# Patch tokens made for all images at the front, and a new order in the attention bodies

## What is computed

```
x = patches(img)                          # 32 x 36 rows of 768
x = layernorm(x) * ln1_g + ln1_b
x = x @ W_lin + b_lin                     # 768 -> 192
x = layernorm(x) * ln2_g + ln2_b
h = concat(cls, x) + pos                  # 37 image tokens an image
h = concat(h, txt)                        # 165 tokens an image
h = h + linear_attention(layernorm(h))    # scores without softmax
h = h + block(layernorm(h))               # 12 heads with softmax, MLP, mixture of 4 experts (top 2)
```

## Time and profile before

| what | value |
|---|---|
| runs, median | 1278.51 us (1276.96 to 1279.22) |
| profiled execution: span | 1279.6 us |
| TensorE (PE) busy | 1201.2 us, 94% |
| VectorE (DVE) busy | 939.3 us, 73% |
| ScalarE (ACT) busy | 730.0 us, 57% |
| GpSimd (POOL) busy | 412.7 us, 32% |

### The profile page before, as it was taken

One profiled execution on the slowest core, in us unless ns is written; L12 is line 12 of the kernel. 1 busy time (PEld: TensorE's weight loads), 2 busy tenths in 40 slices (PEclk: granted clock), 3 DMA queues, 4 the chain that ended last, 5 costly groups with the idle time before them and its releaser, 6 DMA issues.

```text
span 1279.6 us, 28412 instructions
## 1 busy us (share of the span) xinstructions
PE 1201.2 (94%) x9894; PEld 1025.9 (80%) x9894; DVE 939.3 (73%) x2602; ACT 730.0 (57%) x1705; POOL 412.7 (32%) x397
## 2 busy tenths in 40 slices
PE   7899999999999999999998899999999999999994
PEld 6777777777777777777776799998888899899993
DVE  4677787777777787778767678777778877776773
ACT  1256555555566545655557655554656666667661
POOL 2101110111111110111010027877568644455444
PEclk8899999999999999999999999999999999999997
DMA  3481122202120122112400524346477677667652
GB/s 106 122 214 37 38 64 56 64 16 57 56 64 21 51 64 57 39 34 64 96 18 9 206 47 81 79 90 159 118 190 196 169 179 183 164 159 171 183 143 30
DMA packets 95387, 124.51 MB, mean 97 GB/s; under 512 B 9382, under 2 KB 87591, under 8 KB 91343
## 3 DMA queue, kind: packets, MB, share of 16 engines
q1 hardware_dynamic: 71743, 102.48, 26.7%
q0 software_dynamic: 23568, 21.06, 10.9%
HBM read 70.68 MB, written 52.83 MB: 97 GB/s over the span
## 4 chain that ended last, share of the span: by engine, by line
PE 61%; DVE 13%; issue 10%; POOL 5%; DMA 5%; ACT 5%; DVEq 0%; POOLq 0%; SPq 0%; ACTq 0%
PE PS L1634 49%; PE PS L1637 12%; DMA out<-YO,ids 4%; POOL out L769 2%; DVE K L1182 2%; POOL expert_rows L732 1%; DVE st L1094 1%; DVE rec L1204 1%; ACT PT L787 1%; DMA consts<-in_attn_const 1%; ACT XAT L787 1%; ACT GF L980 1%; DVE CN L1205 1%; ACT PX L812 1%; DVE ZS L1152 1%
## 5 line engine op out<-in xcount | busy, mean ns | idle before, releaser
L1634 PE MATMUL PS<-w2r,GH 128*120 (+1 forms) x828 | 247.6, 362 | 2.4 <-DVE GL L1359 1.2
L659 POOL TENSOR_TENSOR rs<-ve,minus_half 128x3 f32<-128x3 f32 (+1 forms) x80 | 58.8, 736 | 558.6 <-DVE ve L1099 558.6
L769 POOL DMA_INDIRECT out<-YO,ids x94 | 160.9, 1712 | 147.0 <-DVE flag L1575 64.0
L1634 PE MATMUL PS<-w2r,GL 128*120 (+1 forms) x828 | 208.0, 251 | 0.0
L812 ACT ACTIVATE PX<-PS,nb 128x165 f32<-128x165 f32 x576 | 177.1, 417 | 47.6 <-DVE nb L1170 45.9
L980 ACT ACTIVATE GF<-PS,b1c 128x480 f32<-128x480 f32 (+1 forms) x216 | 137.8, 638 | 81.9 <-PE PS L1634 79.5
L1634 PE MATMUL PS<-XH,w1r 128*128 128x480 f32 (+1 forms) x432 | 168.9, 393 | 7.2 <-ACT GF L980 4.4
L1634 PEld LDWEIGHTS PS<-w2r,GH 128*120 128x120 f32 x828 | 150.2, 181 | 5.9 <-DVE GL L1359 4.0
L1634 PEld LDWEIGHTS PS<-w2r,GL 128*120 128x120 f32 x828 | 152.4, 184 | 0.0
L1175 DVE COPY PT<-PS 128x384 f32<-128x384 f32 x144 | 80.3, 557 | 87.0 <-PE PS L1637 83.5
L1637 PE MATMUL PS<-ident,PX 128*128 128x128 f32 x864 | 130.5, 281 | 7.3 <-ACT PT L787 5.4
(11 more groups left out here) (270 smaller groups left out, 2332.6 us busy)
## 6 DMA issues: line engine op xcount, KB each, us to landing
w1r<-expert_w_parts SPq DMA_DIRECT2D x25, 1536.0 KB, 7.4
expert_rows<-empty SPq DMA_DIRECT2D x45, 369.4 KB, 5.7
RT<-expert_rows SPq DMA_DIRECT2D x22, 369.4 KB, 3.9
X<-x_scratch SPq DMA_DIRECT2D x11, 360.0 KB, 3.9
out<-X POOLq DMA_DIRECT2D x11, 360.0 KB, 5.6
XP<-in_patches SPq DMA_DIRECT2D x32, 108.0 KB
H<-in_txt SPq DMA_DIRECT2D x16, 192.0 KB, 3.9
out<-H SPq DMA_DIRECT2D x16, 192.0 KB
```

What stands on the lines that cost most here:

```text
L659: nc.gpsimd.tensor_tensor(rs[:, k - 1, 0:n], ve[:, k - 1, 0:n], eps_half[:, 0:n], ALU.pow).then_inc(rstd_ready[k - 1], 1)
L769: nc.gpsimd.indirect_dma_start(out[:, :], bass.IndirectOffsetOnAxis(ap=ids[:, i, t:t + 1], axis=0), YO[:, i % 2, t, :], None, bounds_check ...
L1634: return nc.tensor.matmul(o, l, r, start=start, stop=stop)
```

## The change

The 1152 patch rows of all images are cut into nine full tiles of 128 rows (`PTILES`), which are all worked on in the start-up, in between the steps of pair 0. There are four input buffers (the two old ones and two new) and two for the transposed tile. A tile's mean is subtracted on ScalarE (`centred`), its scale is applied behind the product in `token_stats`, the second normalisation is done by ScalarE (`ynormed`), and GpSimd multiplies by the gain and adds the positions (`patch_tokens`, `positions`). The tokens are stored to a buffer in HBM (`tokd`) and come back with the text, by `load_tokens`, two transfers of 36 rows; pair 0 gets its rows straight from the tile (`first_tokens`). The constants are loaded in two parts each, most of the set-up copies move from VectorE to ScalarE, two memsets to GpSimd, and the weights with the gain multiplied in go to a new tile `wpatch`. Most `keep_running` of the start-up is gone. Bodies 0 to 13 have no patch work any more, body 14 takes the same form as they, and their order is new on TensorE, VectorE and ScalarE; the last body keeps its order. ScalarE's new order of a body is: exps 0, xaT, exps 1, probsT 1, lin_y 0, probsT 3, exps 2, lin_y 1, probsT 5, exps 3, probsT 7, lin_v, lin_m, probsT 9, exps 4, probsT 11, exps 5, probsT 13, 15, 17, contextsT 0 and 1, zT, queries. The list between `h1_store(0)` and `h1_store(1)` is unchanged, but ahead of it now stand the stores of the last four token tiles. Of the diff, the parts that are spoken of:

```diff
+PTILES = B * NPATCH // P
+assert PTILES * P == B * NPATCH
+PBUF = 4
...
-        sp.wait_ge(zeroed, 1)
...
+        def load_patches(t):
+            if t >= PBUF:
+                sp.wait_ge(xnT_ps, t - PBUF + 1)
+            sp.dma_start(XPS[t % PBUF][:, :], a["patches"][P * t:P * t + P, :]).then_inc(patches_in[t % PBUF], 16)
...
+        def load_tokens(i):
+            for b in range(2):
+                sp.dma_start(H[64 * b + 1:64 * b + NIMG, 2, :], tokd[bass.ds((2 * i + b) * NPATCH, NPATCH), :]).then_inc(txt_in, 16)
+        def first_tokens():
+            for b in range(2):
+                sp.dma_start(H[64 * b + 1:64 * b + NIMG, 2, :], TK[NPATCH * b:NPATCH * b + NPATCH, 1, :]).then_inc(txt_in, 16)
+        def store_tokens(t):
+            sp.wait_ge(token_ready, t + 1)
+            if t == 0:
+                first_tokens()
...
-        sp.dma_start(setup_consts[:, :], a["setup_const"]).then_inc(setup_in, 16)
-        sp.dma_start(consts[:, :], a["attn_const"]).then_inc(const_in, 16)
+        sp.dma_start(setup_consts[:, 0:SETUP_FIRST], a["setup_const"][:, 0:SETUP_FIRST]).then_inc(setup_first_in, 16)
+        sp.dma_start(consts[:, 0:CONST_FIRST], a["attn_const"][:, 0:CONST_FIRST]).then_inc(const_first_in, 16)
+        load_patches(1)
+        sp.dma_start(consts[:, CONST_FIRST:], a["attn_const"][:, CONST_FIRST:]).then_inc(const_in, 16)
+        sp.dma_start(TK[:, 0:2, :], a["pos_rows"][:, 0:2, :]).then_inc(pos_in[0], 16)
+        load_text(0)
+        load_patches(2)
+        sp.dma_start(setup_consts[:, SETUP_FIRST:], a["setup_const"][:, SETUP_FIRST:]).then_inc(setup_in, 16)
+        sp.dma_start(TK[:, 2:1 + PTILES, :], a["pos_rows"][:, 2:1 + PTILES, :]).then_inc(pos_in[1], 16)
+        load_patches(3)
         for k in range(2):
             sp.dma_start(ow[64 * k:P, k, :], a["out_wT"][P * k:P * k + KD[k], :]).then_inc(ow_in, 16)
-        load_text(0)
+        for t in range(PTILES - PBUF):
+            load_patches(t + PBUF)
+            store_tokens(t)
         def store_tile(i, src, dst, done):
             sp.dma_start(dst[bass.ds(2 * i, 2), NIMG:S, :].rearrange("b p d -> p b d"), src[:, 0:2, :]).then_inc(done, 16)
...
-            sp.wait_ge(xn_ready, i)
-            load_patches(i)
...
         def x1_store(i):
...
-        next_patches(2)
+        sp.wait_ge(token_stored[0], 32)
         h1_store(0, True)
+        for t in range(PTILES - PBUF, PTILES):
+            store_tokens(t)
...
-        next_patches(3)
+        sp.wait_ge(token_stored[1], 16 * (PTILES - 2))
         h1_store(1, True)
         with sp.Fori(1, PAIRS - 3) as i:
             x1_store(i - 1)
-            next_patches(i + 3)
...
+        def patch_tokens(t):
+            pool.wait_ge(ynorm_ready, t)
+            y = YN[:, t % 3, :]
+            nc.gpsimd.tensor_tensor(y, y, g2, ALU.mult).then_inc(yscaled_ready, 1)
+            pool.wait_ge(yscaled_ready, t)
+            pool.wait_ge(token_ready, t)
+            nc.gpsimd.tensor_tensor(TK[:, 1 + t, :], TK[:, 1 + t, :], y, ALU.add).then_inc(token_ready, 1)
...
+        positions(8)
+        patch_tokens(7)
+        rstd(1, 3, 3)
+        yrstd(8)
+        patch_tokens(8)
...
+        def centred(t):
+            act.wait_ge(mean_ready, t + 1)
+            x = XPS[t % PBUF]
+            nc.scalar.activation(x[:, :], x[:, :], ACT.Identity, bias=pneg[:, t:t + 1], scale=1.0).then_inc(xn_ready, 1)
...
+        zT(0)
+        xnT(8)
+        queries(0)
+        ynormed(7)
+        ynormed(8)
         body(0)
...
+            ts(pve[:, t:t + 1], pmv[:, t, 1:2], EPS, None, ALU.add).then_inc(pvar_ready, 1)
+        def token_stats(t):
+            dve.wait_ge(prstd_ready, t + 1)
+            dve.wait_ge(tok_ps, t + 1)
+            if t > 3:
+                dve.wait_ge(ynorm_ready, t - 3)
+            y = YR[:, t % 3, :]
+            steps.link(stt(y, PS[:, token_bank(t), 0:D], prs[:, t:t + 1], lin_bias[:, :], ALU.mult, ALU.add))
+            steps.link_aggregate(nc.vector.bn_stats(st[:, 1, 0, :], y), pad[:, 0:1])
+            steps.link(nc.vector.bn_aggr(ymv[:, t, :], st[:, 1, 0, :]))
+            ts(yneg[:, t:t + 1], ymv[:, t, 0:1], -1.0, None, ALU.mult)
+            ts(yve[:, t:t + 1], ymv[:, t, 1:2], EPS, None, ALU.add).then_inc(yvar_ready, 1)
...
         def tokens(j):
-            dve.wait_ge(rstd_ready[1], j + 1)
-            steps.link(stt(Y2[:, :], Y[:, :], mv[:, 1, 0, 0:1], g2m[:, :], ALU.subtract, ALU.mult))
-            steps.link(stt(H[:, 2, :], Y2[:, :], rs[:, 1, 0:1], b2m[:, :], ALU.mult, ALU.add))
-            dve.wait_ge(txt_in, j * 16 + 16)
+            dve.wait_ge(txt_in, j * 48 + 48)
             stats(j, 3, lambda t: H[:, t, :], 3)
...
+        def body(i, more=True, first=False):
+            maxima(i, 0)
+            if not first:
+                x1_out(i - 1)
+            lin_in(i + 1)
+            values(i)
+            probsT(i, 0)
+            maxima(i, 1)
+            probsT(i, 2)
+            maxima(i, 2)
+            maxima(i, 3)
+            probsT(i, 4)
+            probsT(i, 6)
+            probsT(i, 8)
+            maxima(i, 4)
+            probsT(i, 10)
+            maxima(i, 5)
+            lin_out(i + 1)
+            probsT(i, 12)
+            probsT(i, 14)
+            u_stats(i + 1, False)
+            probsT(i, 16)
+            z_out(i + 1)
+            contextsT(i)
+            contexts(i, 0)
+            z_low(i + 1)
+            contexts(i, 1)
+            contexts(i, 2)
+            normedT(i)
+            keys(i + 1, 2)
+            keys(i + 1, 1)
+            if not more:
+                w1_low(1)
+            if more:
                 tokens(i + 2)
...
+        keys(0, 1)
+        tokens(1)
+        token_stats(8)
         body(0, first=True)
...
-                pe.wait_ge(h1_ready, j)
+        def patches_T(t):
+            pe.wait_ge(xn_ready, t + 1)
+            if t == 6:
+                pe.wait_ge(ob_ready, 1)
+            elif t > 0:
+                pe.wait_ge(xnT_ready, t - 1 if t == 7 else t)
             for k in range(KP):
...
-            pe.wait_ge(xnT_ready, j + 1)
+        def patch_tokens(t):
+            pe.wait_ge(xnT_ready, t + 1)
+            if t == 0:
+                pe.wait_ge(wpatch_ready, 2)
+            if t >= 2:
+                pe.wait_ge(yvar_ready, t - 1)
+            o = PS[:, token_bank(t), 0:D]
...
+        def body(i, first=False):
+            scores(i, 0)
+            values(i)
+            if first:
+                pe.wait_ge(yvar_ready, PTILES - 1)
+            scores(i, 1, first)
+            transpose_probs(i, 0)
+            if first:
+                pe.wait_ge(yvar_ready, PTILES)
+            transpose_probs(i, 1)
+            tokens_T(i + 1, True)
+            scores(i, 2)
+            transpose_probs(i, 2)
+            lin_y(i + 1, True)
+            transpose_probs(i, 3)
+            scores(i, 3)
+            transpose_probs(i, 4)
+            transpose_probs(i, 5)
+            lin_v(i + 1, 0)
+            transpose_probs(i, 6)
+            transpose_probs(i, 7)
+            lin_v(i + 1, 1)
+            scores(i, 4)
+            scores(i, 5)
+            transpose_probs(i, 8)
+            lin_m(i + 1)
+            transpose_probs(i, 9)
+            transpose_probs(i, 10)
+            lin_tokens(i + 1, 0)
+            lin_tokens(i + 1, 1)
+            transpose_probs(i, 11)
+            transpose_probs(i, 12)
+            transpose_probs(i, 13)
+            transpose_probs(i, 14)
+            transpose_probs(i, 15)
+            contexts_T(i, 0)
+            transpose_probs(i, 16)
+            transpose_probs(i, 17)
+            contexts_T(i, 1)
+            z_T(i + 1)
+            contexts(i, 0)
+            contexts(i, 1)
+            contexts(i, 2)
+            normed_T(i, 0)
+            queries_keys(i + 1, (2,))
+            normed_T(i, 1)
+            normed_T(i, 2)
+            queries_keys(i + 1, (0, 1))
+            project(i)
...
+        lin_tokens(0, 0)
+        lin_tokens(0, 1)
+        output_bias()
+        patches_T(5)
+        patch_tokens(5)
+        patches_T(6)
+        patches_T(7)
+        patch_tokens(6)
+        patch_tokens(7)
+        z_T(0)
+        patches_T(8)
+        pe.wait_ge(attn_const_ready, 1)
+        pe.wait_ge(qk_zeroed, 1)
+        queries_keys(0, (2, 0, 1))
+        patch_tokens(8)
         body(0, first=True)
-        with pe.Fori(1, PAIRS - 2) as i:
```

More of the change, by code:

```diff
@@ L495, in h1_store @@
                 load_text(i + 1)
+                load_tokens(i + 1)
         def x1_store(i):
@@ L667, in residual, with body @@
             last.then_inc(ub_ready, 1)
-        def body(i, lin=True, patch=True, core=True, first=False):
-            if lin:
+        def body(i, lin=True, first=False):
+            if lin and not first:
                 rstd(i + 1, 3, 3)
-            if core:
-                residual(i, first)
-            if patch:
-                rstd(i + 2, 1, 1)
+            residual(i, first)
             if lin:
@@ new lines, in body @@
```

(98 more changed lines are left out.)

652 lines of the change are left out of this document (324 added, 328 removed).

## The result

The changed kernel takes **1295.93 us**, the median of four runs (1293.08 to 1298.35), where the kernel before took 1278.87 in the same set (1276.96 to 1283.13). The ratio is 1.013, with a 95% interval of 1.0109 to 1.0152: slower by 17.1 us. I had forecast 1285.0, or +6.5. The sign was right, the change forecast was less than half of the one measured, and the range (1269 to 1297) only just held it. The time is also one that my third rival would give (1293 to 1300), but not by its way: it wanted the first scores at 73 to 80 us. The profiled execution took 1298.35 us, its span 1296.3.

What follows compares the result with a forecast made beforehand. It read TensorE as holding 61% of the chain of waits and VectorE 13%. The terms -16.5 + 8.1 + 1.5 + 12.4 + 1.0 = +6.5 us, on the runs' median 1278.5, gave 1285.0 us; range 1269 to 1297.

Steps and rivals of the forecast that it cites:

- third rival: Start-up bound by VectorE and GpSimd: first scores at 73 to 80 us, total 1293 to 1300; chance 0.15.
- Part 1: Bodies 0 to 14: patch removal and the new order make the period 40.37 us, -16.5 us in all.
- part 4: SyncE's late list makes VectorE wait for pair 2's tokens: +12.4 us once, plus 1.0 for TensorE's clock.
- Part 2: Start-up with all patch tiles: first scores of body 0 at 65.5 us, +8.1 us (bounds +4 and +15).
- The port rule: Start-up: VectorE two-port and GpSimd instructions exclude each other; 25 GpSimd operations would cost VectorE up to 15 us.
- Part 3: Body 0: ScalarE waits for GpSimd in ynormed(8) with exps 0 behind it, a loss of 1.5 us.
- S: The start of the first scores of body 0, from which times were counted; forecast at 65.5 us.
- The rival in which the queue does not bite: SyncE's backlog or list goes faster: 13.4 us fall away, total 1271.6 us, faster; chance 0.17.
- The order opens PE: Bodies: TensorE's waits mostly go, period towards 38.5 us; half way, 39.4, total 1271, fully 1259; chance 0.13.
- the period of 40.4: Sign: bodies 2 to 13 each take 40.4 us; a period under 40 would prove the prediction wrong.
- faster: Outcome of the whole kernel beyond the 0.2% a measurement can tell from no change; chance 0.28.

Runs made afterwards that it cites:

- e2: Changed kernel with contexts_T(i, 0) moved ahead of transpose_probs(i, 14) on TensorE; 1281.37 us, ratio 1.0016 to the kernel before.
- e3: Changed kernel with 14 useless filler matmuls in TensorE's wait ahead of transpose_probs(i, 14); 1279.84 us, ratio 0.9995 to the kernel before.
- e10: e1 with VectorE's copy of group 12 moved ahead of H1's statistics, TensorE's new order untouched; ratio 0.989 to the kernel before.
- e8: e6 with keys(i+1, 2) put ahead of normedT(i) again on VectorE; ratio 0.9923 to the kernel before.
- e4: Changed kernel with the old body order back on TensorE, VectorE and ScalarE, patches still at the front; 1285.86 us, ratio 1.0053 to the kernel before.
- e7: e6 with 40 idle transposes put into TensorE's idle times of the start-up; ratio 0.988 to the kernel before.
- e9: e7 with ynormed(8) behind exps 0 of body 0 on ScalarE; ratio 0.9856 to the kernel before.
- e11: e9 with the copy of tile 12 moved inside lin_out as in e10; ratio 0.9854 to the kernel before.
- e12: e11 with the fills behind H1's store and pair 2's loads in SyncE's queue; 1259.27 us against 1278.82, ratio 0.9847.
- e6: Changed kernel with the edits of e1 and e2 together; ratio 0.9881 to the kernel before.
- e1: Changed kernel with SyncE's last token stores (tiles 5 to 8) moved behind the list of small loads; 1279.79 us, ratio 1.0004 to the kernel before.
- e5: Kernel before with one wait so that SyncE's list starts when body 0's first probabilities are ready; ratio 1.0116 to the kernel before.

## Why the prediction was right and wrong

**Part 1, the bodies: the step that failed.** I wrote that TensorE stands about 1.8 us ahead of group 14 and does `contexts_T(0)` afterwards, "ending level with Z", and priced the order at 0.27. The wait was 1.83. At full clock Z's transposes come 31.8 us into the body (I had 31.2 to 31.5), and the period is 39.92, better than my 40.37. But I carried TensorE's durations across the wait unchanged, though in part 4 I had charged the clock for a wait of 12 us and had the earlier trace rows to show that an idle of 1.65 us is enough: 0.50 in the window behind it. In the body shown the six transposes and the contexts behind the wait take 1.24 + 3.14 us instead of 0.88 + 1.89, and the body ends 1.5 us later. So the bodies, forecast at -16.5, gave that back in part: the surplus of bodies 2 to 14 is 8.8 us. e2, e3 and e10 each removed the idle time in another way, and all three give 39.8 to 39.95 in every body of the loop. Which bodies escape I could not have said, nor can I now.

A second, smaller miss went the other way: I priced the swap of `normedT` and `keys` at nothing, and it gives 0.27 a body (e8). It was named in no step. The 0.27 that I charged for the order was not there either: e8, the new order without the swap and with its clock kept, takes 40.20, e4 in the old order 40.19.

**Part 2, the start-up: mechanism right, size short.** The tokens landed and were read at 21.07 (forecast 21.3), `tokens_T(0)` came at 25.40 (24.9). Then TensorE's clock fell twice and I had charged none of it. With the clock mostly kept, the first scores come at 61.7 to 63.5 in e7, e9, e11 and e12, under my 65.5. In kernels whose start-up is the changed kernel's own they lie between 62.98 (e4) and 67.6 (e3), so a single profile says this number to some 2 us only. Much of that is there before TensorE begins: the tokens are read at 18.75 (e4) to 21.35 (e3). From that reading to the first scores it is 44.2 to 46.3 us in these kernels, and 41.6 to 43.8 in the four with their idle transposes back.

The port rule did not decide. VectorE's XA beside GpSimd took 1.86 us for three operations, where the earlier trace rows make 1.1 alone and 1.9 at the slower rate. With the clock mostly kept the whole start-up is 4.3 to 6.1 us longer than before, though all of the GpSimd operations are still there. The Trainium skill, "SBUF — State Buffer", section "Who interferes with whom", says that the later of the two fully blocks, which I had turned into up to 15 us by an estimate; a start-up longer by as much was in no run. How much of the 4.3 to 6.1 us is this contention was not tried.

**Part 3, body 0: right mechanism, size 1.0 for 1.5.** ScalarE waited 2.97 us in `ynormed(8)` and exps 0 began 3.86 us behind the first scores, where I had S + 3.9. Body 0 still took 40.09 and not 41.9. In e9, e11 and e12, where the wait is gone, it takes 39.11 by its first scores, so the term was worth 1.0 (0.8 in e6, whose body 0 takes 39.90); the rest of the miss is a body 0 that without it is 1.3 us shorter than my 40.37. Why it is also 0.8 shorter than a steady body was not tried. The 3.1 us between e7 and e9 are more than the term, since in e7 the clock fell behind the wait.

**Part 4, the queue: right.** The list started at S + 5.7 (forecast 5.6), the text of pair 2 went out at S + 47.3 (45.4), and VectorE waited 13.7 us (12.4). e1 removes the wait and e5 makes it in the kernel before. Body 1 lost 56.79 - 39.92 = 16.9 in all, of which 3.2 is not the wait. Without the stall (e1) the body takes 41.14, since the clock falls in it as in the others; so about 2.0 belong to the clock behind the stall, where I had 1.0 (the scores behind it took 2.02 for 1.11). The rival in which the queue does not bite fell.

**The rival on TensorE.** "The order opens PE" gave 38.5 to 39.4. No run came under 39.8 in the loop. That fits VectorE's chain H1, U, Z, which no run shortened and which the earlier trace rows had set against this rival.

**Signs and sums.** Of the signs that I named, VectorE's wait on `H`, the first vector 5.7 us behind the first scores and TensorE's idle times ahead of `transpose_probs(14)` (1.83) and `tokens_T` (0.49) were there; the period of 40.4 was not. Two sums were off: "faster" was given 0.28 where the first two rivals alone make 0.30, and the lower gain of part 1 is 11.6, not 11. Neither changes the forecast.

What stays open: why the same wait of 1.83 us sometimes leaves the clock alone, and how much VectorE and GpSimd cost each other in the start-up.

## What to carry to other kernels

Here a wait that hid behind another engine was free only where TensorE kept its clock. Wherever an order leaves TensorE idle for 1.5 to 2 us as here, price the work behind it at the half clock too, once per loop body. Fill such a gap with work that is due anyway (e2), or remove its source by moving one copy (e10). Before you delay something in an in-order transfer queue, add up what stands behind it and ask when the first of those is wanted; and expect the queue to come back as the limit once the engines are faster (e9).

## What the runs showed of the hardware that was not expected

- Every one of twelve bodies of one execution has the same idle time of 1.83 or 1.84 us; nine of them lose 1.3 to 1.6 us to a lower clock behind it and three lose nothing. Waits of 1.25 us once a body (e2, e4, e6) left the periods even and at their full-clock length.
- The same kernel before took 1287.61 us in one set and 1278.82 to 1279.53 in the others. Inside stage one the traces of that set agree with the others' (41.55 us a body in e5 and in the kernel before, 39.93 in e6 against 39.92 in e2). What is longer is stage two: from the last copy of the values to the end e5 to e8 take 602 to 606 us, all other kernels 594.7 to 598.2. The cause stays open.
